# First stage of a convolution kernel taken from image strips, in 32x32 TensorE tiles

## The reference

```python
x = x + L0(_gn(x))
x = x + L1(_gn(x))

def L0(x):                      # a and b: two branches of 16 channels each
    fa, fb = _bn(_conv(x, conv_a_w, conv_a_b, pad=1)), _bn(_conv(x, conv_b_w, conv_b_b, pad=1))    # 3x3
    att_a = _bn(_conv(concat([fa, gh, gw]), att_a_w, att_a_b))          # 1x1, one channel
    map_a = sigmoid(_conv(concat([att_a, gh, gw, pr]), attn_a_w, pad=1))  # 3x3, one channel
    ...                                                                  # att_b, map_b alike
    return concat([fa * (map_a * scale1), fb * (map_b * scale2)])
```

## Time and profile before

| what | us |
|---|---|
| median of 3 runs (range) | 419.23 (417.98 to 421.49) |
| profiled execution, first to last instruction | 422.3 |
| of it, start to the first matmul of the convolution | 23.97 |
| start to the second normalisation (L1211) | 81.26 |
| from there to the end | 341.0 |

### The profile page before, as it was taken

One profiled execution on the slowest core, in us unless ns is written; L12 is line 12 of the kernel. 1 busy time (PEld: TensorE's weight loads), 2 busy tenths in 40 slices (PEclk: granted clock), 3 DMA queues, 4 the chain that ended last, 5 costly groups with the idle time before them and its releaser, 6 DMA issues.

```text
span 422.3 us, 14389 instructions
## 1 busy us (share of the span) xinstructions
PE 318.9 (76%) x6057; PEld 207.0 (49%) x6058; DVE 326.1 (77%) x641; ACT 248.1 (59%) x364; POOL 204.2 (48%) x244
## 2 busy tenths in 40 slices
PE   0079999858858409999889989888999889993570
PEld 0022334312213105777767767667777677772460
DVE  5456258833599842999999999989999799997266
ACT  1023323305136205888868888878888688884355
POOL 9770000199491000566654665656666366867000
PEclk9999999969588555999999999999999899997565
DMA  7799200188570634300110101001110000000005
GB/s 224 134 234 232 57 2 0 31 210 246 130 194 5 127 88 102 93 8 28 30 27 3 48 29 28 29 4 47 28 28 8 25 3 3 7 19 2 3 0 199
DMA packets 18106, 28.65 MB, mean 68 GB/s; under 512 B 6890, under 2 KB 7465, under 8 KB 18029
## 3 DMA queue, kind: packets, MB, share of 16 engines
q1 hardware_dynamic: 12397, 19.40, 17.4%
q0 software_dynamic: 2400, 5.07, 5.3%
q10 hardware_dynamic: 3246, 3.27, 3.5%
HBM read 8.03 MB, written 5.83 MB: 33 GB/s over the span
## 4 chain that ended last, share of the span: by engine, by line
PE 43%; ACT 26%; DVE 10%; DMA 7%; SPq 7%; issue 6%; POOL 1%; DVEq 1%; ACTq 1%; POOLq 0%
ACT hx L936 16%; PE ps L645 10%; PE ps L776 9%; ACT zreg L1019 7%; PE ps L588 6%; PE ps L609 5%; PE ps L658 4%; DMA hx<-xpad 3%; SPq L443 3%; PE ps L785 2%; SPq L347 2%; DVE prod L1318 2%; PE ps L599 2%; DMA x_sb<-in_x 1%; DVE x_sb L1413 1%
## 5 line engine op out<-in xcount | busy, mean ns | idle before, releaser
L564 POOL TENSOR_TENSOR prod<-prod 128x416 f32<-128x416 f32 x128 | 134.9, 1076 | 122.2 <-DVE prod L1318 122.2
L1318 DVE TENSOR_TENSOR prod<-ps,hy 128x480 f32<-128x480 f32 (+1 forms) x256 | 137.8, 600 | 14.8 <-PE ps L785 12.2
L785 PE MATMUL ps<-zreg,hx 64*64 64x96 f32 x4608 | 115.5, 250 | 0.0
L936 ACT ACTIVATE hx<-ps 128x576 f32<-128x576 f32 x131 | 78.2, 648 | 49.1 <-PE ps L776 31.6
L785 PEld LDWEIGHTS ps<-zreg,hx 64*64 64x64 f32 x4608 | 103.3, 135 | 7.6 <-issue 0.2
L1023 ACT ACTIVATE hx<-hx,rbias 128x1152 f32<-128x1152 f32 x64 | 81.1, 1267 | 0.0
L1326 DVE TENSOR_REDUCE areg<-prod 128x32 f32<-128x448 f32 x128 | 72.8, 608 | 0.5 <-POOL prod L564 0.4
L645 PE MATMUL ps<-preg,sel 26*128 26x288 bf16 x260 | 43.1, 284 | 31.3 <-ACT zreg L1019 17.8
L776 PE MATMUL ps<-wzp,sreg 128*128 128x144 bf16 x512 | 43.6, 229 | 0.0
L645 PEld LDWEIGHTS ps<-preg,sel 26*128 26x128 bf16 x260 | 20.1, 92 | 47.2 <-issue 29.4
L1019 ACT ACTIVATE zreg<-ps 128x576 f32<-128x576 f32 x64 | 42.1, 658 | 0.0
(11 more groups left out here) (178 smaller groups left out, 359.4 us busy)
## 6 DMA issues: line engine op xcount, KB each, us to landing
scratch<-zreg SPq DMA_DIRECT2D x12, 240.0 KB, 4.3
sreg<-scratch SPq DMA_DIRECT2D x12, 192.0 KB, 2.5
out<-x_sb SPq DMA_DIRECT2D x8, 256.0 KB, 2.1
x_sb<-in_x SPq DMA_DIRECT2D x3, 512.0 KB, 5.0
areg<-xpad POOLq DMA_DIRECT2D x23, 66.0 KB, 3.9
areg<-xpad SPq DMA_DIRECT2D x23, 66.0 KB, 2.9
sreg<-scratch SPq DMA_DIRECT2D x4, 336.0 KB, 3.3
zreg<-xpad POOLq DMA_DIRECT2D x15, 66.0 KB, 4.1
```

What stands on the lines that cost most here:

```text
L564: pool.tensor_tensor(slots[:, :, 0:2 * moved], slots[:, :, 0:2 * moved], slots[:, :, 2 * KEPT:6 * KK], ALU.add).then_inc(folded, 1)
L785: return pe.matmul(g_ps(g, h)[u * W:(u + 1) * W, k - TAPS[h][0], :, :], hx[s, (t + u) % 4, k, :], z_sb[s, y + u + k // 3:y + u + k // 3 + ...
L936: act.activation(hx[:, t % 4, :, :].rearrange("p k (h x) -> p h k x", h=2), dist_ps(bank).rearrange("p h (k x) -> p h k x", k=KK), ACT.Abs)\
L1318: mul = vector.tensor_tensor(pv[:, n0:n1], gv, wv[:, n0:n1], ALU.mult)
```

## The change

Nothing is copied within SBUF any more. `load_strips` loads the image from HBM a second time, as four strips of 16 rows with a row of margin on either side (18 rows): partition `32*j + c` of `xraw` holds channel `c` of strip `j`, and the four images lie along the free dimension. SP loads strips 0 and 1, ACT strips 2 and 3, images 0 and 1 ahead of images 2 and 3; each of the eight transfers is 272 to 295 KB. `x_sb` is still loaded, behind them, for the residual. Since a channel's pixels now lie in four partition groups, the moments are taken per strip and image and averaged over the strips by two small matmuls with `avg4`. DVE writes `xstrip` in two halves (10 and 8 rows, `norm1`).

`conv_half` runs all nine taps as matmuls of 32x32 weights over 512 pixels, 16 per tap: tile position `(j*C, b*C)`, strip `j` in the rows of the array, image `b` in its columns, and strip `j` into PSUM bank `4*h + j`. Its order is taps, strips, images. That makes 144 matmuls in each half, 288 in all, in the place of 96. ACT's eight saves (into the same `f_sb`, now with a row of margin) follow. The attention is three pieces of four column tiles (`att_piece`), saved once each by DVE with the position images added. `map_pair` computes the map on 8 rows of each 32-row group only (2 strips x 4 quarter strips x 9 taps = 72 matmuls of 256 pixels a pair, 12 rows contracted), the sigmoid runs on these, two instructions in all, and `spread_pair` copies the rows to 128 partitions by a matmul with a 0/1 matrix, 8 matmuls of 128 columns per pair. DVE then reads the map from PSUM and works on 1024 pixels at a time. In the diff, which is cut, `STRIPS` is 4, `SROWS` 16, `LROWS` 18, `QROWS` 4 and `SLEN` 1024:

```diff
-        attrep = zflat[0:GRP_ROWS, 0:AR * AR].rearrange("p (r x) -> p r x", x=AR)
+        attrep = zflat[:, 0:LROWS * XC].rearrange("p (r x) -> p r x", x=XC)
+        posrep = zflat[:, LROWS * XC:2 * LROWS * XC].rearrange("p (r x) -> p r x", x=XC)
+        xstrip = zflat[:, 2 * LROWS * XC:(2 + B) * LROWS * XC].rearrange("p (b r x) -> p b r x", b=B, x=XC)
...
+        def load_strips(eng, strips, pair):
+            x_c = d["x"].rearrange("(b c) n -> c b n", b=B)
+            for j in strips:
+                l0, l1 = (1 if j == 0 else 0), (LROWS - 1 if j == STRIPS - 1 else LROWS)
+                r0 = j * SROWS - 1
+                eng.dma_start(xraw[j * C:(j + 1) * C, 2 * pair:2 * pair + 2, l0 * W:l1 * W],
+                              x_c[:, 2 * pair:2 * pair + 2, (r0 + l0) * W:(r0 + l1) * W])\
+                    .then_inc(x_loaded[pair], 16)
...
+            sync.wait_ge(xraw_zeroed, 2)
+            load_strips(sync, (0, 1), 0)
+            load_strips(sync, (0, 1), 1)
+            for j in range(STRIPS):
+                sync.dma_start(w0[j * C:(j + 1) * C, :, :], d["w0"]).then_inc(w0_loaded, 16)
+            for i in range(2):
+                half = slice(i * NPIX // 2, (i + 1) * NPIX // 2)
+                sync.dma_start(x_sb[:, half], d["x"][:, half]).then_inc(xnat_loaded, 16)
...
-            for c in range(NCH):
-                sync.wait_ge(norm1, (c + 1) // 2 + 1)
-                replicate(sync, c, SYNC_ROWS, xrep, xrep_ready)
...
-            sync.wait_ge(sig_used, NCH + CREDIT)
+            sync.wait_ge(x1_ready, STRIPS)
...
-            def conv_chunk(c, u):
-                pe.wait_ge(xrep_ready[c], 16 * (len(SYNC_ROWS) + len(ACT_ROWS)))
-                pe.wait_ge(xrep_last[c], 16 * len(POOL_ROWS))
-                rows = xrep[c].rearrange("p b (r x) -> p b r x", x=XC)
-                for dx in range(3):
-                    for b in range(B):
-                        mm = pe.matmul(ps[b * C:(b + 1) * C, u * BANK:(u + 1) * BANK], w0[:, dx, :],
-                                       rows[:, b, :, dx:dx + W], start=dx == 0, stop=dx == 2,
-                                       tile_position=(0, b * C))
-                mm.then_inc(conv_ready, 1)
...
+            pe.wait_ge(avg_loaded, 16)
+            pe.wait_ge(smean_in, B)
+            moments = small[:, SMV:SMV + 2 * B].rearrange("p (b s) -> p s b", s=2)
+            pe.matmul(ps[:, 0:B], avg4[:, :], moments[:, 0, :], start=True, stop=True).then_inc(smean_ready, 1)
+            pe.wait_ge(svar_in, 1)
+            pe.matmul(ps[:, BANK:BANK + B], avg4[:, :], small[:, SDIF:SDIF + B], start=True, stop=True)\
+                .then_inc(svar_ready, 1)
+            def conv_half(h):
+                pe.wait_ge(norm1, (h + 1) * (B + 1))
+                for k in range(KK):
+                    dy, dx = k // 3, k % 3
+                    for j in range(STRIPS):
+                        for b in range(B):
+                            mm = pe.matmul(ps[b * C:(b + 1) * C, (4 * h + j) * BANK:(4 * h + j + 1) * BANK],
+                                           w0[j * C:(j + 1) * C, k, :],
+                                           xstrip[j * C:(j + 1) * C, b, h * CH_ROWS + dy:(h + 1) * CH_ROWS + dy,
+                                                  dx:dx + W],
+                                           start=k == 0, stop=k == KK - 1, tile_position=(j * C, b * C))
+                        if k == KK - 1:
+                            mm.then_inc(conv_ready, 1)
+            def att_piece(p):
+                for q in range(STRIPS):
+                    mm = pe.matmul(ps[q * C:(q + 1) * C, p * BANK:p * BANK + LROWS // 3 * W], attw[:, :],
+                                   f_sb[:, (q * SROWS + p * (LROWS // 3)) * W:(q * SROWS + (p + 1) * (LROWS // 3)) * W],
+                                   start=True, stop=True, tile_position=(0, q * C))
+                mm.then_inc(att_ready, 1)
...
+            def map_pair(pair):
+                for k in range(KK):
+                    dy, dx = k // 3, k % 3
+                    for q in (2 * pair, 2 * pair + 1):
+                        rows = slice(q * C, q * C + NATT + NPOS)
+                        for s in range(4):
+                            mm = pe.matmul(ps[s * C:(s + 1) * C, (4 + q) * BANK:(4 + q) * BANK + QROWS * W],
+                                           mapw[rows, k, :],
+                                           attrep[rows, s * QROWS + dy:(s + 1) * QROWS + dy, dx:dx + W],
+                                           start=k == 0, stop=k == KK - 1, tile_position=(q * C, s * C))
                 mm.then_inc(map_ready, 1)
-            conv_chunk(0, 0)
+            def spread_pair(pair):
+                pe.wait_ge(sig_ready, pair + 1)
+                for i in range(2):
+                    for s in range(4):
+                        rows = slice(s * C, s * C + NATT)
+                        at = (4 * pair + s) * BANK + i * QROWS * W
+                        mm = pe.matmul(ps[:, at:at + QROWS * W], spread[rows, :], sig[rows, 2 * pair + i, :],
+                                       start=True, stop=True, tile_position=(s * C, 0))
+                    mm.then_inc(gate_ready, 1)
+            pe.wait_ge(w0_loaded, 16 * STRIPS)
+            conv_half(0)
+            conv_half(1)
             pe.wait_ge(attw_ready, 1)
-            for c in range(NCH - 1):
-                pe.wait_ge(f_ready, c + CREDIT)
-                conv_chunk(c + 1, (c + 1) % 2)
-                att_chunk(c, c % 2)
-                if c == 2:
-                    pe.wait_ge(mapw_ready, 1)
-                    pe.wait_ge(pos_loaded, 16 * 3)
-                if c >= 2:
-                    map_chunk(c - 2, c % 2)
-            att_chunk(NCH - 1, 1)
-            for c in range(NCH - 3, NCH):
-                map_chunk(c, c % 2)
+            pe.wait_ge(f_ready, NCH)
+            for p in range(3):
+                att_piece(p)
+            pe.wait_ge(mapw_ready, 1)
+            pe.wait_ge(att_saved, 3)
+            map_pair(0)
+            map_pair(1)
+            pe.wait_ge(spread_ready, 1)
+            spread_pair(0)
+            spread_pair(1)
...
+            pe.wait_ge(gated_ready, 2)
...
+            load_strips(act, (2, 3), 0)
+            act.dma_start(avg4[:, :], d["avg4"]).then_inc(avg_loaded, 16)
+            load_strips(act, (2, 3), 1)
...
+            for h in range(2):
+                for j in range(STRIPS):
+                    at = (1 + j * SROWS + h * CH_ROWS) * W
+                    act.wait_ge(conv_ready, h * STRIPS + j + 1)
+                    act.activation(f_sb[:, at:at + BANK], ps[:, (4 * h + j) * BANK:(4 * h + j + 1) * BANK],
+                                   ACT.Identity, bias=col(BB), scale=col(BS)).then_inc(f_ready, 1)
+            for pair in range(2):
+                act.wait_ge(map_ready, pair + 1)
+                act.activation(sig[:, 2 * pair:2 * pair + 2, :],
+                               ps[:, (4 + 2 * pair) * BANK:(6 + 2 * pair) * BANK]
+                               .rearrange("p (q n) -> p q n", q=2)[:, :, 0:QROWS * W], ACT.Sigmoid)\
                     .then_inc(sig_ready, 1)
...
+            vector.memset(xraw[0:C, :, 0:W], 0.0).then_inc(xraw_zeroed, 1)
+            vector.memset(xraw[P128 - C:P128, :, (LROWS - 1) * W:LROWS * W], 0.0).then_inc(xraw_zeroed, 1)
+            vector.memset(warm[:, :], 1.0).then_inc(warm_in, 1)
...
+            for b in range(B):
+                if b % 2 == 0:
+                    vector.wait_ge(x_loaded[b // 2], 16 * STRIPS)
+                for i in range(2):
+                    vector.bn_stats(stats[:, 2 * b + i, :], xraw[:, b, W + i * BANK:W + (i + 1) * BANK])\
+                        .then_inc(st_ready, 1)
+            for b in range(B):
+                vector.wait_ge(st_ready, 2 * b + 2)
+                vector.bn_aggr(small[:, SMV + 2 * b:SMV + 2 * b + 2], stats[:, 2 * b:2 * b + 2, :]).then_inc(smean_in, 1)
+            moments = small[:, SMV:SMV + 2 * B].rearrange("p (b s) -> p s b", s=2)
+            dif, smean, srstd = small[:, SDIF:SDIF + B], small[:, SMEAN:SMEAN + B], small[:, SRSTD:SRSTD + B]
+            vector.wait_ge(smean_in, B)
+            vector.wait_ge(smean_ready, 1)
+            chain(vector.tensor_tensor(dif, moments[:, 0, :], ps[:, 0:B], ALU.subtract))
+            chain(vector.tensor_tensor(dif, dif, dif, ALU.mult))
+            vector.tensor_tensor(dif, dif, moments[:, 1, :], ALU.add).then_inc(svar_in, 1)
+            chain(vector.tensor_copy(smean, ps[:, 0:B]))
+            vector.wait_ge(svar_ready, 1)
+            rstd(srstd, ps[:, BANK:BANK + B], GN_EPS)
             inner = xpad[:, PAD_T:PAD_T + H, 1:1 + W]
             x3 = x_sb[:, :].rearrange("p (y x) -> p y x", y=H)
-            ends = [0] + [min((2 * i + 1) * CH_ROWS + 1, H) for i in range(NORM1)]
-            for r0, r1 in zip(ends[:-1], ends[1:]):
-                vector.tensor_scalar(inner[:, r0:r1, :], x3[:, r0:r1, :], col(MV), col(RSTD),
```

(45 more changed lines are left out.)

250 lines of the change are left out of this document (87 added, 163 removed).

## The result

The changed kernel takes 424.79 us (median of 15 runs, 421.59 to 431.47) against 419.96 for the kernel before in the same series (15 runs): ratio 1.0094, 95% interval 1.0067 to 1.0120. Forecast were 409.7 us and a range of 402 to 418. Some executions of a kernel run slower than its others, the profiled one of the changed kernel among them: every ratio in this document leaves those out, every median and range takes them in. The profiled execution took 428.79 us, 4.0 above the median.

A forecast was written before the change was run, and what follows sets the result against it. TensorE was taken to bound the first stage from 23.97 us on; load, convolution, attention, map and adds summed to a second normalisation at 71.7 instead of 81.26, 9.5 us off the median of 419.23: 409.7 us, range 402 to 418.

The forecast's parts named there:

- I take 0.36, the nearest row with the same source and destination memories: Strip load: transfers at 0.36 MB/us, so the second pair of images is in at 10.8 us.
- lower bound: Strip load: slowest rate expected, the copies' 232 GB/s to 32 partitions, strips in at 14.2 us.
- 3.4 us later: Strip load: the delay of the 2.36 MB at 232 GB/s, against 0.36 MB/us.
- rival 3: Strip load at 232 GB/s: 3.4 us later, 413.1 us; 0.23 together with rival 1 (414 to 423).
- SP's and ACT's strips fill different partitions at once: Strip load: the argument given against rival 3, whose rate is 232 GB/s.
- At up to 0.7 each they end by 13.5: ACT's queue: seventeen transfer issues end by 13.5 us, 2 us before the root is asked for.
- cold start: Convolution's beginning: PE comes cold as before, adding 2.1 us (2.06) to its time.
- if all sixteen tiles run so: Convolution: every tile takes an instruction each 452 ns, one per 28 ns overall, both halves 16.3 us.
- rival 2: Convolution: row groups of 32 overlap in pairs only, costing 16.3 us; 6.8 slower, 426.0 us; chance 0.08.
- rival 1: Convolution: tiles fill worse, 40 ns an instruction, 23.0 us, time 416.4; 0.23 together with rival 3 (414 to 423).
- So I take 2.1: Pause of 3 us between convolution and attention: price of a lowered clock, set between 0 and 2.1 us.
- The adds and what follows: Adds 14.4 us, then 1.6 to the second normalisation at 71.7; from there 341 us to the end, as now.

The follow-up runs named there:

- e13: Changed kernel with only strips and avg4 transferred until the strips are in, ScalarE's small loads behind the first root: 420.23 us, ratio 0.9998.
- e14: Changed kernel, strips laid out beforehand for 128 partitions, nothing transferred beside them, root first, 32-row map, spare matmuls before the convolution: 413.02 us, ratio 0.9726.
- e11: Changed kernel with the eight strip transfers on three queues instead of two: 423.32 us, ratio 1.0065.
- e2: Changed kernel with strips laid out beforehand in device memory, outside the timed kernel, each transfer filling 128 partitions: 420.41 us, ratio 1.0013.
- e3: Changed kernel with ScalarE issuing the eight attt loads behind its first root: 421.58 us, ratio 1.0071.
- e7: Changed kernel with the convolution's images in the outer and strips in the inner loop: 423.27 us, ratio 1.0094.
- e4: Changed kernel with the map's matmuls contracting all 32 rows of their group, 20 of them zeros: 420.13 us, ratio 0.9982.
- e10: Changed kernel with the convolution in pieces of 256 columns, twice the instructions: 442.44 us, one run.
- e16: Same as e14, but with x_sb back right behind the weights instead of behind all tables: 408.78 us, ratio 0.9741.
- e17: Same as e15, but with x_sb right behind the weights: 417.16 us, ratio 0.9899.
- e15: Changed kernel, nothing but avg4 transferred beside the strips, x_sb late, root first, 32-row map, spare matmuls before the convolution: 418.45 us, ratio 0.9936.

## Why the prediction was wrong

The shape of the sum was right, and its parts behind the map were met; three terms were mis-sized and one was put in the wrong place.

1. **The load: 6.3 of the 12.9 us.** The step that failed is "I take 0.36, the nearest row with the same source and destination memories". Nearest was the row with the same number of partitions, the copies' 232 GB/s, which the prediction had as its lower bound: e13 gives 14.09 where that bound said 14.2, and e14 shows that 0.36 holds for 128 partitions (10.07 against 10.8). (The bound's "3.4 us later" comes out at 3.6, 2.36/0.232 less 2.36/0.36, so 14.4.) So rival 3 was the case, and "SP's and ACT's strips fill different partitions at once" was no reason against it: a third queue brought nothing (e11). The other 3.0 us were in no case: the sum had only `avg4` beside the strips, not the weights, the tables and `x_sb` that the same queues issue next.
2. **The root: 1.2.** "At up to 0.7 each they end by 13.5" carried SyncE's 0.5 us an issue over to ScalarE's seventeen (there are eighteen). The eight `attt` loads took 2.1 us each to issue, with the DMA engines' share near 1.00; in e14, where they are issued at shares of 0.08 to 0.31, 0.7 each (5.79 us in all). Their last was out at 23.4, 1.3 us behind the request for the root. In e2, with the strips 4.0 us sooner, the issues ended 4.1 sooner and the root still waited 1.52. e3 gives the 1.3 back.
3. **The convolution: 3.1.** The cold start was nearly right (2.6 against 2.06). The step that failed is "if all sixteen tiles run so": 33 ns an instruction instead of 28, 2.7 us. Why 33 is open; e7 excludes the order. The 24.6 ns of L785, which seemed to leave room for 28, belong to instructions of 96 columns, not 512. That is still 13.7 times as fast as one tile after another at 452 ns, so rival 2's limit to pairs is refuted, and rival 1's 40 ns was too slow. The Trainium skill's 10.6-fold ("TensorE: Matmul & The Clock Gate", "Part 3: Packing small matmuls — row/col tiling") gave an estimate of 24.6 us; the trace has 19.0.
4. **The clock: charged at the wrong place, and for too little.** "So I take 2.1" laid the fall to the pause of 3 us. In the changed kernel's profile the pause kept 1.00; the clock fell in the map instead, which cost 3.8 us there (12.4 against 8.6) and 1.0 in the spreading, while 8.0 and 1.2 in e4 confirm what the prediction had for full speed. No case had a busy TensorE losing its clock. The Trainium skill ("TensorE: Matmul & The Clock Gate", "Why this matters for your kernels") lays drops to idle gaps between bursts; the trace disagrees here, since TensorE was busy from 53.95 on without a gap when the clock fell, at 56.7; in e10 and e16, where it fell within the pause, the traces agree.
5. **The adds and what follows: right, the second by luck.** 16.1 us against 16.0, in every profile alike. 342.3 to the end against 341 is one execution; the others' 335.1 to 341.5 go beyond the 2 us that the prediction allowed this stretch.

With load and root mended, the map on 32 rows and the cold start covered, the kernel comes out near the forecast: e16's stage is 70.4 against 71.7, its time 408.78 against 409.7. That is luck in part: the cold start that e16 does not pay (2.1 in the sum) makes up for most of the slower pace of the convolution (2.7). The wrong part was not the idea of the sum but the rates in it, and all errors but one made it too short. (The pause, charged with 2.1, was the one that ran the other way.)

## What to carry to other kernels

Take the rate of a transfer from a row with the same number of partitions, and add what the same and other queues issue beside it. Where matmuls use few rows of a tile, contract over zero rows as well: that costs no instruction and kept the clock here, in seven of the eight profiles that have it (in e17 the clock had fallen ahead of the map and did not return in it). And a transfer moved out of the way must land somewhere: look at what runs there, TensorE's instructions included.

## What the runs showed of the hardware that was not expected

- The granted clock fell to 0.50 under a TensorE that was busy in every microsecond, with 12 of 32 rows in each tile; with 32 rows, zeros in 20 of them, it stayed at 1.00 (e4).
- Transfers to 32 partitions ran at 190 to 247 GB/s with the DMA engines' share at 0.93 to 1.06, the same bytes in rows of the same length, in transfers twice as large, to 128 partitions at 407 to 426 (e13, e14).
- With 21.6 ns an instruction, TensorE stopped for about 1 us behind every 128 of them (e10); and a 2 MB transfer beside the convolution brought it to a stop of 0.95 to 1.32 us (e14, e15) that went away when the transfer was moved (e16, e17). The packets of the "instruction" queue, whose starts precede the end of each of these stops by 2.3 to 2.7 us, speak for the loading of its instructions; no edit tested that by itself.
